# Last layer's partial results: stores split by halves of the partitions, the on-chip half laid out in pairs of groups, and two weight loads issued later

## The chip, the cores and the metric

The kernel runs on one core of a Trainium2 chip. The metric is the device time of one execution in microseconds (us); lower is better. Before the change the median of 3 runs is 1939.19 us (1938.2 to 1945.02).

The engines are TensorE (PE in the profile; PEld is its weight load), VectorE (DVE), ScalarE (ACT), GpSimd (POOL) and SyncE (SP). In this kernel SP issues nearly all transfers between HBM and on-chip memory, and 16 DMA engines carry them out.

## The reference

The input is x, 16 x 256 x 256 float32, that is 4096 tokens of 256 features. Four layers add to it in turn: a cross attention with a hard choice, a mixture of 8 experts, a cross attention with 16 heads of 64, and the one that matters here, a grouped mixture of 32 x 4 = 128 small experts:

```
b, s, d = x.shape                                   # 16, 256, 256, normalized x
g = Wc.shape[1]                                     # 32
grouped = x.reshape(b, s // g, g, d)                # 128 groups of 32 tokens
logits = einsum('bntd,des->bntes', grouped, Wc) + bc + tie
perm = (logits == max(logits, axis=-3))             # each of 128 experts picks one token of each group
permuted = einsum('bntd,bntes->bnesd', grouped, perm)
inner = relu(einsum('bnesd,esdf->bnesf', permuted, W1) + b1)       # 256 -> 32
result_permuted = einsum('bnesf,esdf->bnesd', inner, W2) + b2      # 32 -> 256
result = einsum('bnesd,bntes->bntd', result_permuted, perm)        # back to the tokens
```

## The kernel before, in words

The first 1680 us or so compute the three earlier layers. The last layer follows as one long stage.

*Choice and gather* (`pe_step`, with `dve_step`, `act_step`, `pool_step`). For each of 16 batches of 256 tokens the experts' choices are found (PMT), and TensorE gathers the chosen tokens into PX. The 128 groups of tokens fall into two halves, 64 groups each. The first half's up products run in the middle of it.

*Up products* (`pe_up`, `dve_up`). Four products per half (j = 0 to 3, 32 experts each), with W1 in the four buffers WF1P. Each signals `s_u3`, so that `s_u3` counts to 4 for the first half and to 8 for both. The result after ReLU is INT.

*Down products* (`pe_tail`). For k = 0 to 7, `down_a(k)` computes the first half's results of 16 of the 128 experts and `down_b(k)` computes the second half's results, again for 16 experts. `down_a` has groups on the partitions, `down_b` features. VectorE and ScalarE, two PSUM banks each, copy `down_a`'s result to RPA (two buffers, 1 MiB each) and `down_b`'s result to RPB (64 KiB per partition, one buffer for all k). `s_e0` and `s_e1` count these copies. `down_a(k)` waits for the RPA copies of k-1, `down_b(k)` for the RPB copies of k-1. The copy into RPA for k waits until the store of k-2 has landed (`rpa_free`).

*The way out and back for the first half.* SP stores each RPA to the scratch tensor `rpd` (64 groups, 128 experts, 256 features). A partition of RPA holds, for one of 64 groups and one of two values of a, 8 experts x 256 features, which is 8 KiB in one piece in `rpd`. Partition 64a + g is group g. The store is one transfer of 128 partitions whose destination is written as a (2), g (64), 2048 elements. After all eight stores have landed SP loads R2A(b), b = 0 to 7, with experts on the partitions, 1 MiB each, three buffers.

*The way for the second half.* RPB stays on chip, and `turn_b` transposes it, with experts on the partitions afterwards; VectorE adds b2 into R2B.

*Return* (`bias`, `back`, `out_add`, SP's `out`). TensorE brings the results back to the tokens, VectorE adds them to X, and SP stores 16 pieces of the output, 256 KiB each. The program of TensorE for i = 0 to 9 is: `turn_b(i)`, `bias(i-2)`, `back("b", i-1)`, `back("a", i-2)`, as far as these exist.

*W2.* WF2P[0 to 3] hold W2, 1 MiB each; `down_a(k)` and `down_b(k)` use WF2P[k // 2]. WF2P[2] and WF2P[3] lie where WF1P[0] and WF1P[1] were. SP's program (`sp_tail`) issues loads 0 and 1 after the last gather (`s_ga` 16), load 2 at `s_u3` 5, load 3 at `s_u3` 6, and then the stores of RPA.

The order of each engine's work is its program text, written out by hand; waits are on semaphores and nothing is reordered. Where a line of the profile names L28, it is the helper `Waits.wait_ge`.

Of the kernel before, what the change touches and what calls it, by code (L numbers as in the profile page):

```python
# [56 lines left out]
def build(nc, A, OUT):  # L57
    fp32 = mybir.dt.float32
# [8 lines left out]
    def sem(name):  # L67
        return nc.alloc_semaphore(name)
# [3 lines left out]
    PS = [nc.alloc_psum_tensor(f"ps{i}", [128, 512], fp32) for i in range(8)]  # L72
# [9 lines left out]
    rpd = nc.dram_tensor("rp_scratch", (64, 128, 256), fp32).ap()  # L82
# [4 lines left out]
    ident, ustrict, ones = CST[:, 0:128], CST[:, 128:256], CST[:, 256:384]  # L87
# [226 lines left out]
    for i in range(SLOTS0):  # L314
        g, r = i // 8, i % 8
# [35 lines left out]
    d_ks_rp = [sem(f"d_ks_rp{i}") for i in range(4)]  # L351
# [1063 lines left out]
    attn_at = mem.at  # L1415
# [73 lines left out]
    WF1P += [Arena(nc, ot1_at + 8192 * i)(f"WF1P{i + 2}", [128, 2, 32, 32], fp32) for i in range(2)]  # L1489
    RPA = [Arena(nc, ot1_at + 8192 * i)(f"RPA{i}", [128, 2, 4, 256], fp32) for i in range(2)]  # L1490
    PX = Arena(nc, attn_at)("PX", [128, 2, 128, 64], fp32)
    RPB = Arena(nc, attn_at)("RPB", [128, 2, 64, 128], fp32)

    d_c1 = sem("d_c1")
    d_wf1, d_wf2 = [sem(f"d_wf1{i}") for i in range(2)], [sem(f"d_wf2{i}") for i in range(2)]
# [4 lines left out]
    s_px, s_py, s_u3, s_in, s_b2 = sem("px_act"), sem("px_dve"), sem("upmm3"), sem("inner3"), sem("b2split")  # L1500
    s_fm, s_e0, s_e1, s_cm2, s_xo = sem("downmm3"), sem("rp0"), sem("rp1"), sem("returnmm"), sem("xout")
    TURN, LOGIT, PERM, GATHER, SMALL = PS[0], PS[1], PS[2], (3, 4, 5, 7), (0, 1, 2, 6)
    ks_sent = 32 * 16
# [12 lines left out]
    def returned(kind, b):  # L1516
        return RET.index((kind, b)) + 1

    def rpa_free(w, k):
        if k >= 2:  # L1520
            w.wait_ge(d_ks_rp[(k - 2) % 4], ks_sent + 16 * ((k - 2) // 4 + 1))

    def rpa_part(k, r):
        return RPA[k % 2][:, :, r, :], PS[SMALL[r]][:, :].rearrange("p (h d) -> p h d", h=2)

    def rpb_part(k, r):
        es = 16 * (4 * (k % 2) + k // 2) + r
        return (RPB[:, :, :, :].rearrange("p a g s -> p s (a g)")[:, es:es + 13:4, :],
                PS[GATHER[r]][:, :].rearrange("p (q n) -> p q n", q=4))

    def pe_step(e, w, n):
        def turn_choice(b):
# [73 lines left out]
    def pe_tail(e, w):  # L1606
# [37 lines left out]
        def turn_b(i):  # L1644
            for t in range(4):
                w.wait_ge(s_e0, 16)
                w.wait_ge(s_e1, 16)
                w.wait_ge(s_e0, 16 + 4 * (i - 1) + t + 1 if i else 16)
                for u in range(2):
                    for dh in range(2):  # L1650
                        c0 = u * 256 + dh * 128
                        m = e.transpose(PS[SMALL[t]][:, c0:c0 + 128], RPB[:, dh, 8 * i + 2 * t + u, :], ident)
                m.then_inc(s_fm, 1)

        def bias(b):
# [31 lines left out]
        for i in range(10):  # L1687
            if i < 8:
                turn_b(i)
            if i >= 2:  # L1690
                bias(i - 2)
            if 1 <= i <= 8:
                back("b", i - 1)
            if i >= 2:
                back("a", i - 2)
# [73 lines left out]
    def dve_tail(e, w):  # L1769
# [9 lines left out]
        for k in range(8):  # L1779
            w.wait_ge(s_fm, 2 * k + 1)  # L1780
            rpa_free(w, k)
            for r in range(2):
                i = e.tensor_copy(*rpa_part(k, r))
            i.then_inc(s_e0, 1)
            w.wait_ge(s_fm, 2 * k + 2)
            for r in range(2):
                i = e.tensor_copy(*rpb_part(k, r))
            i.then_inc(s_e0, 1)
# [27 lines left out]
    def act_tail(e, w):  # L1816
        w.wait_ge(s_om, 32)
        w.wait_ge(s_u3, 8)
        for k in range(8):
            w.wait_ge(s_fm, 2 * k + 1)  # L1820
            rpa_free(w, k)
            for r in range(2, 4):
                i = e.activation(*rpa_part(k, r), ACT.Copy)
            i.then_inc(s_e1, 1)
            w.wait_ge(s_fm, 2 * k + 2)
            for r in range(2, 4):
                i = e.activation(*rpb_part(k, r), ACT.Copy)
            i.then_inc(s_e1, 1)
# [17 lines left out]
    def sp_tail(e, w):  # L1846
        def first(j, buf):
            sent = d_kl_wf1[buf] if buf < 2 else d_wf1[j]
            e.dma_start(WF1P[buf][:, :, :, :], A["wf1"][:, :, 32 * j:32 * j + 32, :]).then_inc(sent, 16)

        def second(j):
            sent = d_wt_wf2[j] if j < 2 else d_wf2[j - 2]
            e.dma_start(WF2P[j][:, :, :].rearrange("p (a q) d -> p a q d", a=2),
                        A["wf2"].rearrange("p (a q) d -> p a q d", a=2)[:, :, 4 * j:4 * j + 4, :]).then_inc(sent, 16)

        def out(kind, b):
            n = returned(kind, b)
            t, m = 2 * (b + 8 * (kind == "b")), (n - 1) % 4
            w.wait_ge(s_xo, n)
            e.dma_start(o_v[:, t:t + 2, :], XO[m][:, :, :]).then_inc(d_x_wf2_out[m], 16)  # L1860

        def back_in(b):
            w.wait_ge(s_cm2, returned("a", b - NR) if b >= NR else 0)
            e.dma_start(R2A[b % NR][:, :, :], rpd[8 * b:8 * b + 8, :, :].rearrange("n s d -> s n d")).then_inc(d_r2[b % NR], 16)

        w.wait_ge(s_ca, 64)
        e.dma_start(WC1[:, :, :], A["wc1"]).then_inc(d_c1, 16)
        e.dma_start(BC1[:, :], A["bc1"]).then_inc(d_c1, 16)
        e.dma_start(B1[:, :], A["b1_1"]).then_inc(d_c1, 16)
        w.wait_ge(a1.s_sc, 2 * U)  # L1870
        e.dma_start(B2[:, :], A["b2_1"]).then_inc(d_c1, 16)
        first(0, 0)
        first(1, 1)
        w.wait_ge(s_om, 32)
        first(0, 2)
        first(1, 3)
        w.wait_ge(s_u3, 1)
        first(2, 0)
        w.wait_ge(s_u3, 2)
        first(3, 1)  # L1880
        w.wait_ge(s_ga, 16)
        second(0)
        second(1)
        w.wait_ge(s_u3, 5)
        second(2)
        w.wait_ge(s_u3, 6)
        second(3)
        for k in range(8):
            w.wait_ge(s_e0, 2 * k + 1)
            w.wait_ge(s_e1, 2 * k + 1)  # L1890
            e.dma_start(rpd.rearrange("g (a k y) d -> k a g (y d)", a=2, k=8)[k],
                        RPA[k % 2][:, :, :, :].rearrange("p h r d -> p (h r d)")).then_inc(d_ks_rp[k % 4], 16)
        for j in range(4):
            w.wait_ge(d_ks_rp[j], ks_sent + 16 * 2)
        w.wait_ge(s_fm, 16)
        for b in range(NR):
            back_in(b)
        for kind, b in RET:
            if kind == "a" and b + NR < 8:
                back_in(b + NR)  # L1900
            out(kind, b)
        for j in range(4):
            w.wait_ge(d_x_wf2_out[j], 16 + 16 * 4)
# [513 lines left out]
```

## Time and profile before

| what | us |
|---|---|
| median of 3 runs | 1939.19 (1938.2 to 1945.02) |
| the profiled execution's own time | 1944.29 |
| its span, first to last instruction | 1942.4 |
| TensorE matmul busy | 1717.9 (88%) |
| DVE busy | 1314.3 (68%) |
| ACT busy | 1153.3 (59%) |
| POOL busy | 822.2 (42%) |

The profile shows one execution of the program. All positions in it are microseconds from the first instruction. The granted clock of TensorE is given as a share of full speed (1.00 is 2.4 GHz, 0.50 is 1.2 GHz). "DMA share" is the mean busy share of the 16 DMA engines. Transfers are not counted as engine work: an engine that waits for one shows as idle, with the transfer named as the releaser. A float32 matmul whose operands are not transposes shows as two records.

### The profile page before, as it was taken

What the parts mean: (1) busy time and instruction counts of PE and PEld (TensorE: products, weight loads), DVE (VectorE), ACT (ScalarE), POOL (GpSimd) and SP (SyncE); (2) the same over time, 40 slices, a digit from 0 to 9 for tenths busy, and PEclk for the clock granted to TensorE, in tenths of its full rate; (3) what the DMA queues carried; (4) which work ended last, traced back from release to release, by engine and by line L of the source; (5) the groups of instructions that cost most, each with busy time, mean ns of one, the idle gap of its engine ahead of it and who ended that gap; (6) DMA issues with size and microseconds to landing.
All of it is one profiled execution on the core that took longest, in us unless ns stands there. A gap on an engine that the chain in (4) does not pass through costs nothing.

```text
span 1942.4 us, 42261 instructions
## 1 busy us (share of the span) xinstructions
PE 1717.9 (88%) x16368; PEld 1470.4 (76%) x16368; DVE 1314.3 (68%) x2802; ACT 1153.3 (59%) x2882; POOL 822.2 (42%) x1292
## 2 busy tenths in 40 slices
PE   5899999999999999999997999999999999773235
PEld 4567676788999999999996787887887887662123
DVE  4798988427058988888866777777777766641124
ACT  1477776333467777777755777777777774331100
POOL 2244532100123333333316778888888775320000
PEclk7799999999999999999998999999999999875567
DMA  6756554368766666666765222222222111221117
GB/s 176 216 116 140 120 133 96 115 220 290 255 232 245 230 235 247 251 237 230 243 239 174 63 66 88 66 67 88 66 66 88 56 53 47 89 93 54 54 54 269
DMA packets 130553, 285.02 MB, mean 147 GB/s; under 512 B 13681, under 2 KB 74353, under 8 KB 116657
## 3 DMA queue, kind: packets, MB, share of 16 engines
q1 hardware_dynamic: 110768, 174.00, 29.4%
q0 software_dynamic: 19584, 108.31, 16.1%
q8 instruction: 130, 2.13, 0.4%
q14 instruction: 71, 0.57, 0.1%
HBM read 199.95 MB, written 82.05 MB: 145 GB/s over the span
## 4 chain that ended last, share of the span: by engine, by line
PE 70%; DMA 11%; DVE 10%; POOL 4%; issue 4%; ACT 1%; SPq 0%; DVEq 0%; POOLq 0%; ACTq 0%
PE ps L1250 11%; PE ps L1236 11%; DMA rp_scratch<-RPA 8%; PE ps L1928 5%; PE ps L373 4%; PE ps L219 4%; PE ps L1959 4%; PE ps L1914 4%; PE ps L1948 4%; PE ps L379 3%; PE ps L464 2%; PE ps L440 2%; DVE NM L592 2%; POOL P L209 2%; PE ps L540 2%
## 5 line engine op out<-in xcount | busy, mean ns | idle before, releaser
L196 ACT ACTIVATE P<-ps,NM 128x256 f32<-128x256 f32 x512 | 236.7, 482 | 126.5 <-DVE NM L185 125.8
L209 POOL TENSOR_TENSOR P<-P,RS 128x1024 f32<-128x1024 f32 x128 | 243.1, 1904 | 72.1 <-DVE RS L203 71.6
L1236 PE MATMUL ps<-XRP,W1P 128*128 128x256 f32 x1872 | 226.8, 281 | 3.3 <-DVE W1P L1319 3.3
L1236 PEld LDWEIGHTS ps<-XRP,W1P 128*128 128x128 f32 x1872 | 220.1, 190 | 3.6 <-DVE W1P L1319 3.6
L1250 PE MATMUL ps<-W2P,HP 128*128 128x256 f32 x1872 | 221.5, 277 | 0.0
L1250 PEld LDWEIGHTS ps<-W2P,HP 128*128 128x128 f32 x1872 | 218.0, 188 | 0.0
L592 DVE TENSOR_REDUCE NM<-ps 128x2 f32<-128x512 f32 x256 | 164.3, 684 | 33.4 <-PE ps L440 32.3
L690 ACT ACTIVATE PT<-ps 128x512 f32<-128x512 f32 x256 | 139.2, 597 | 66.3 <-PE ps L452 63.8
L185 DVE TENSOR_REDUCE NM<-ps 128x2 f32<-128x512 f32 x256 | 164.5, 684 | 5.7 <-PE ps L1914 4.2
L1170 POOL DMA_INDIRECT WE<-in_we,WIX x39 | 44.3, 1137 | 269.2 <-DVE W1P L1319 208.8
L1279 ACT ACTIVATE HF<-ps,WE 128x256 f32<-128x256 f32 x312 | 129.1, 465 | 43.0 <-PE ps L1236 43.0
L2047 DVE CAST OT<-ps 128x256 fp32r<-128x256 f32 x128 | 54.3, 424 | 139.0 <-PE ps L1928 137.7
L1914 PEld LDWEIGHTS ps<-K,Q 64*128 64x128 f32 x1536 | 100.9, 189 | 59.7 <-issue 42.4
L226 ACT ACTIVATE PT<-ps 128x512 f32<-128x512 f32 x256 | 140.9, 618 | 0.7 <-PE ps L219 0.7
L1928 PE MATMUL ps<-PT,V 128*64 128x256 f32 x1024 | 138.8, 392 | 1.1 <-DVE OT L2049 1.1
L1914 PE MATMUL ps<-K,Q 64*128 64x256 f32 x1536 | 127.4, 299 | 10.6 <-DVE Q L2041 5.4
L219 PE MATMUL ps<-CST,P 128*128 128x128 f32 x1024 | 133.0, 273 | 3.1 <-ACT PT L226 3.1
L1270 ACT ACTIVATE W2P<-WE 128x512 fp32r<-128x512 f32 x156 | 97.2, 623 | 53.9 <-PE ps L1250 53.9
L1166 POOL DMA_INDIRECT XR<-xn_scratch,RIX x78 | 79.6, 1020 | 102.1 <-PE ps L1212 48.1
L219 PEld LDWEIGHTS ps<-CST,P 128*128 128x128 f32 x1024 | 114.4, 140 | 4.6 <-issue 3.9
L1336 DVE TENSOR_TENSOR HP<-HF,HP 128x512 fp32r<-128x512 f32 x156 | 108.0, 692 | 13.3 <-ACT HP L1286 7.1
L1948 PE MATMUL ps<-XNP,W1Q 128*128 128x256 f32 x768 | 110.4, 294 | 4.5 <-POOL XNP L2221 4.5
(234 smaller groups left out, 3765.0 us busy)
## 6 DMA issues: line engine op xcount, KB each, us to landing
KS<-k_scratch SPq DMA_DIRECT2D x64, 256.0 KB, 3.1
V<-v_scratch SPq DMA_DIRECT2D x16, 1024.0 KB, 6.3
k_scratch<-KVM SPq DMA_DIRECT2D x52, 256.0 KB
QS<-q_scratch SPq DMA_DIRECT2D x96, 128.0 KB, 4.6
v_scratch<-KVM SPq DMA_DIRECT2D x40, 256.0 KB
ys_scratch<-YS SPq DMA_DIRECT2D x39, 256.0 KB, 7.9
ctx_scratch<-CHL SPq DMA_DIRECT2D x32, 256.0 KB, 3.0
CHR<-ctx_scratch SPq DMA_DIRECT2D x16, 512.0 KB, 4.5
```

Of the source, the lines that this page charges most:

```text
L185: e.tensor_reduce(self.NM[:, u % 4, 2 * x:2 * x + 2], PS[SB[n % 3]][:, :].rearrange("p (h j) -> p h j", h=2), AX.X, ALU.max, negate=True). ...
L196: i = e.activation(self.P[u % 4][:, c, :], PS[SB[n % 3]][:, y * 256:y * 256 + 256], ACT.Exp, bias=self.NM[:, u % 4, c:c + 1], accum_out=se ...
L209: e.tensor_tensor(p, p, self.RS[:, u % 4, :].unsqueeze(2).to_broadcast([128, 4, 256]), ALU.mult).then_inc(self.s_pn, 1)
L219: i = e.transpose(PS[TB[h]][:, c0:c0 + 128], self.P[u % 4][:, c, jt * 128:jt * 128 + 128], ident)
L226: e.activation(self.PT[u % 4][h][:, :], PS[TB[h]][:, :], ACT.Copy).then_inc(self.s_tv, 1)
L592: e.tensor_reduce(NM0[b % 2][:, :, 8 * h + p], PS[SB[(2 * u + h) % 3]][:, :].rearrange("p (l j) -> p l j", l=2), AX.X, ALU.max, negate=Tru ...
L690: e.activation(PT0[u % 4][h][:, :], PS[TB[h]][:, :], ACT.Exp).then_inc(s_ex0, 1)
L1236: m = e.matmul(PS[p][:, hh * 256:hh * 256 + 256], W1P[i % 2][wi][:, cc * 1024 + hc * 128:cc * 1024 + hc * 128 + 128], XRP[i % 2][xi][:, cc ...
L1250: m = e.matmul(PS[4 + k][:, s * 256:s * 256 + 256], HP[k][hi][:, hc, s * 128:s * 128 + 128], W2P[k][wi][:, hc * 256:hc * 256 + 256], start ...
L1914: m = e.matmul(PS[SB[(2 * u + h) % 3]][:, lt * 256:lt * 256 + 256], Q1[i][64 * h:64 * h + 64, p, lt * 128:lt * 128 + 128], K1[j][64 * h:64 ...
L1928: m = e.matmul(PS[OB][64 * h:64 * h + 64, 0:256], V1[b % 2][:, jt, (2 * p + h) * 64:(2 * p + h) * 64 + 64], a1.PT[u % 4][h][:, jt * 256:jt ...
L1948: m = e.matmul(QB[:, j * 256:j * 256 + 256], W1Q[wi][:, cc, c0:c0 + 128], XNP[b % 2][xi][:, cc, :], start=(cc == 0 and x == 0), stop=(cc = ...
```

## The change

Three edits, all in the last layer. Each RPA store becomes two transfers, one for each half of the 128 partitions (a = 0, then a = 1), with groups as the outermost dimension of the destination; the semaphore targets go from 16 to 32 for each k. RPB holds the two groups 2n and 2n + 1 side by side for each expert (last dimension y), so that `rpb_part` writes and `turn_b` reads with other steps. SP's loads of WF2P[2] and WF2P[3] both wait for `s_u3` 8.

```diff
-    RPB = Arena(nc, attn_at)("RPB", [128, 2, 64, 128], fp32)
+    RPB = Arena(nc, attn_at)("RPB", [128, 2, 32, 128, 2], fp32)
@@ def rpa_free(w, k)
-            w.wait_ge(d_ks_rp[(k - 2) % 4], ks_sent + 16 * ((k - 2) // 4 + 1))
+            w.wait_ge(d_ks_rp[(k - 2) % 4], ks_sent + 32 * ((k - 2) // 4 + 1))
@@ def rpb_part(k, r)
-        return (RPB[:, :, :, :].rearrange("p a g s -> p s (a g)")[:, es:es + 13:4, :],
-                PS[GATHER[r]][:, :].rearrange("p (q n) -> p q n", q=4))
+        return (RPB[:, :, :, :, :].rearrange("p a g s y -> p s (a g) y")[:, es:es + 13:4, :, :],
+                PS[GATHER[r]][:, :].rearrange("p (q n y) -> p q n y", q=4, y=2))
@@ def turn_b(i)
-                        m = e.transpose(PS[SMALL[t]][:, c0:c0 + 128], RPB[:, dh, 8 * i + 2 * t + u, :], ident)
+                        m = e.transpose(PS[SMALL[t]][:, c0:c0 + 128], RPB[:, dh, 4 * i + t, :, u], ident)
@@ def sp_tail(e, w)
-        w.wait_ge(s_u3, 5)
+        w.wait_ge(s_u3, 8)
         second(2)
-        w.wait_ge(s_u3, 6)
         second(3)
         for k in range(8):
             w.wait_ge(s_e0, 2 * k + 1)
             w.wait_ge(s_e1, 2 * k + 1)
-            e.dma_start(rpd.rearrange("g (a k y) d -> k a g (y d)", a=2, k=8)[k],
-                        RPA[k % 2][:, :, :, :].rearrange("p h r d -> p (h r d)")).then_inc(d_ks_rp[k % 4], 16)
+            for a in range(2):
+                e.dma_start(rpd[:, 64 * a + 8 * k:64 * a + 8 * k + 8, :].rearrange("g y d -> g (y d)"),
+                            RPA[k % 2][64 * a:64 * a + 64, :, :, :].rearrange("p h r d -> p (h r d)")).then_inc(d_ks_rp[k % 4], 16)
         for j in range(4):
-            w.wait_ge(d_ks_rp[j], ks_sent + 16 * 2)
+            w.wait_ge(d_ks_rp[j], ks_sent + 32 * 2)
```

## Rows read from the trace of the kernel before

**Rows 1.** The page: the chain that ended last, share of the span by engine.
```profile
PE 70%; DMA 11%; DVE 10%; POOL 4%; issue 4%; ACT 1%; SPq 0%; DVEq 0%; POOLq 0%; ACTq 0%
```

**Rows 2.** The chain in order of time, 1743 to 1908: start us, us, what.
```profile
1743.85 2.45 DVE RPB L1787 x2
...
1747.44 37.01 DMA rp_scratch<-RPA
1784.54 1.30 DVE RPA L1783 x2
...
1864.19 37.76 DMA rp_scratch<-RPA
1902.09 5.89 DMA R2A<-rp_scratch
1908.03 1.94 PE ps L1678 x16
```

**Rows 3.** Windows of 4 us; columns in the first line.
```profile
core 0: us, PE busy (x) PEld busy (x) DVE busy (x) ACT busy (x) POOL busy (x), PEclk, DMA share, GB/s
...
1724.00:1728.00 4.00, 2.25 (x85) 2.01 (x79) 1.12 (x2) 0.00 (x0) 0.00 (x0) 0.50 1.01 378
...
1732.00:1736.00 4.00, 1.20 (x88) 1.03 (x76) 1.12 (x2) 0.00 (x0) 0.00 (x0) 1.00 0.64 247
...
1740.00:1744.00 4.00, 4.00 (x113) 2.90 (x116) 2.56 (x5) 1.24 (x3) 0.00 (x0) 0.97 0.02 4
1744.00:1748.00 4.00, 2.39 (x72) 1.93 (x59) 3.41 (x4) 3.21 (x4) 0.00 (x0) 0.89 0.13 49
1748.00:1752.00 4.00, 3.53 (x63) 2.28 (x60) 2.36 (x2) 2.37 (x2) 0.00 (x0) 0.50 0.13 53
...
1776.00:1780.00 4.00, 0.00 (x0) 0.00 (x0) 0.00 (x0) 0.00 (x0) 0.00 (x0) 0.50 0.13 53
1868.00:1872.00 4.00, 4.00 (x32) 3.67 (x34) 3.68 (x6) 0.00 (x0) 0.00 (x0) 0.75 0.13 53
1920.00:1924.00 4.00, 4.00 (x52) 2.94 (x51) 3.67 (x6) 0.00 (x0) 0.00 (x0) 1.00 1.09 379
```

**Rows 4.** Line 1045, the four 1 MiB stores of `XNF`: time to landing.
```profile
DMA to landing us min/median/max: 4.9/6.0/7.1
```

**Rows 5.** Timeline from 1720: start, length, engine, line, operation, shapes, count, idle before.
```profile
1726.91 3.44 PE L1602 MATMUL ps<-PX,WF1P 128*32 128x64 f32 x128 [1.75 <-issue]
...
1731.21 1.99 PE L1602 MATMUL ps<-PX,WF1P 128*32 128x64 f32 x128 [0.85 <-issue]
...
1737.16 2.99 PE L1602 MATMUL ps<-PX,WF1P 128*32 128x64 f32 x101 [3.96 <-issue]
...
1741.77 2.01 PE L1640 MATMUL ps<-INT,WF2P 32*128 32x64 f32 x64
...
1743.20 43.14 SPq L1891 DMA_DIRECT2D rp_scratch<-RPA  x4
...
1766.30 2.01 PE L1626 MATMUL ps<-WF2P,INT 32*64 32x256 f32 x32 [10.37 <-DVE RPA L1783]
...
1768.24 3.69 PE L1640 MATMUL ps<-INT,WF2P 32*128 32x64 f32 x64
```

**Rows 6.** Groups by shape, 1676 to 1943: busy us, mean ns, idle before.
```profile
L1787 DVE COPY RPB<-ps 128x512 f32<-128x512 f32 x16 | 16.3, 1098 | 2.9 <-PE ps L1640 2.9
...
L1783 DVE COPY RPA<-ps 128x512 f32<-128x512 f32 x16 | 10.3, 688 | 95.8 <-DMA rp_scratch<-RPA 95.2 <-PE ps L1626 0.5
...
L1709 DVE COPY PX<-ps 128x512 f32<-128x512 f32 x9 | 6.2, 687 | 7.2 <-PE ps L1571 7.2
```

**Rows 7.** Timeline from 1862, the transposes (line 1652) and the adds.
```profile
1865.99 5.63 PE L1652 MATMUL ps<-CST,RPB 128*128 128x128 f32 x32 [15.72 <-DVE RPB L1787]
...
1874.92 1.07 PE L1678 MATMUL ps<-R2B,PMT 128*32 128x256 f32 x16
...
1918.84 1.97 PE L1652 MATMUL ps<-CST,RPB 128*128 128x128 f32 x16
```

## The prediction

> **What bounds the kernel now.** I read four views, from wide to narrow. The page's chain by engine comes first: TensorE carries 70% and DMA 11% [rows 1]. TensorE's share is spread over the whole kernel, the DMA share is nearly all in one place. The chain in order of time shows that place: from 1743.20 to 1902.09 us it is one long alternation of `rp_scratch<-RPA` waits of 37 to 38 us and copies of 1.3 us [rows 2] (the first store's issue at 1743.20 is in [rows 5]). (A 37 us piece spans two of the eight stores: RPA has two buffers, so the copy of group k waits for the store of k-2.) Each store then takes (1902.09 - 1743.20) / 8 = 19.9 us for 1 MiB. The windows say why [rows 3]: with nothing else running, at 1776, the DMA engines are 0.13 busy and move 53 GB/s. 0.13 of 16 engines is 2 engines, at some 27 GB/s each. TensorE does nothing in that window. So this stage waits for two DMA engines, and the other fourteen are idle.
>
> The Trainium skill ("DMA: Bandwidth & Descriptors", section on why a DMA increments its semaphore by 16) says that the number of engines is the largest up to 16 that divides the slowest dimension of both sides. The destination here has a=2 outermost. The 0.13 agrees with 2 of 16.
>
> **Edit 1, each store as two of 64 partitions.** The outermost dimension becomes 64 on both sides. If that lets all engines work, a group's megabyte no longer takes 19.9 us. Bounds for issue to landing of 1 MiB: below, 4.9 us, the fastest of the four other 1 MiB stores of this kernel (`xn_scratch<-XNF`; 4.9/6.0/7.1) [rows 4]; above, the 19.9 us of now. Nothing in the trace shows a big transfer on 64 partitions. The nearest row is the 1 MiB store, and I take its slow end, 7.1, less a little: 7.0, issue of the second half (0.48 us, one more SP issue per group) included. SP has nothing else to do there, so eight more issues cost nothing.
>
> With stores at 7 us the loop has another bound, its own pace per group, c. Down product "b" of group k+1 waits for the RPB copies of group k, and these for product b of group k. At full clock: product b 2.01 us (the one at 1741.77), two RPB copies, handoffs of about 0.2 [rows 5]. At half clock TensorE alone takes 2.01 + 3.69 + 0.1 = 5.8 us a group (the pair at 1766.30 and 1768.24) and that hides the copies.
>
> **Edit 2, RPB in pairs of groups.** The copy now writes two neighbouring floats at each stop and not one. Now a DVE copy takes 1.10 us against 0.69 for the contiguous RPA copy. The trace has a row for writes in pairs: the PX copies (line 1709) write pairs far apart and take 0.687 us [rows 6]. Bounds 0.69 and 1.10; I take 0.69, its exact likeness. Two copies 1.4 us, so at full clock c = 2.01 + 1.4 + 0.2 = 3.6; with the old layout, whose first copies took 2.45 us [rows 2], it would be 4.7. The price is on the reading side: 128 transposes now read with a step of two floats. No row shows such a read. Not below now (same elements, same shape); above, I bound it by twice, 1.97 us more per group of 16 [rows 7]. I take nothing, and keep the other end as a rival.
>
> Which clock? TensorE's granted clock was 0.97 at 1740, 0.89 at 1744 with TensorE busy 2.39 of 4 us, and 0.50 from 1748 (0.50 is 1.2 GHz, 1.00 is 2.4 GHz); in 1868:1872, after TensorE had begun to work without a pause at 1866, it was back at 0.75, and it is 1.00 at 1920 [rows 3]. At c = 3.6 TensorE would be busy 3.1 of 3.6 us, far more than in the window before it fell; if it does fall, it is busy without a pause and may rise again. So c lies between 3.6 and 5.8, with a mix likely. Middle 4.7; I take 4.9, since the only two groups that ran undisturbed did lose the clock.
>
> Does the store fit under 4.9? RPA's copy of k+2 would like to start 2 x 4.9 - 1.3 = 8.5 us after the issue of store k; landing takes 7.0. 1.5 us to spare; each us beyond costs half a us a group, 3.5 in all.
>
> The Trainium skill has a rule against this edit ("SBUF — State Buffer", Door 1, the DMA port swizzle; also "DMA: Bandwidth & Descriptors", table of patterns): partitions 0 to 63 reach only 8 of the 16 memory ports, two transfers to the two halves serialize, and one should use one transfer of 128 partitions. By its 218 GB/s a group would take an estimated 4.8 us of transfer, just under my pace. No row here shows the 64-partition case.
>
> **Edit 3, W2 loads 2 and 3 wait for all up products.** Now the third and fourth load (1 MiB each) are issued during up products, and TensorE then stands with "issue" as the cause: 1.75 us before 1726.91 (first loads in flight, stays) and 3.96 before 1737.16, with 0.85 between these two [rows 5]. In 1732:1736 TensorE had 1.20 us of work while DMA moved 247 GB/s. 0.85 + 3.96 = 4.8 us is the most that goes. But SP now issues both loads as the down products start (2 x 0.6 us, done before the first store is due 3.1 us later), and TensorE still has to get its instructions while 2 MiB move, for some 6 us at the 378 GB/s of 1724:1728 [rows 3]. Part of the stall comes back there. Bounds: gain 4.8, loss 3. I take a gain of 2.0. The loads land some 8 us after the up products; group 4 needs them after 4 x 4.9 = 20 us. Store 0 queues behind them, and lands about 11 us after the down products start, where its buffer is wanted after 3.1 + 8.5 = 11.6: covered by 0.6 us.
>
> **The sum**, on the profiled execution (span 1942.40, its own time 1944.29):
> first store issued at 1743.20 - 2.0 = 1741.2; eighth 7 x 4.9 = 34.3 later, 1775.5 (now 1864.19); landed + 7.0 = 1782.5; first R2A load + 5.9 = 1788.4; then what follows 1908.0 now, 34.4 us to the end [rows 2], 1822.8. The 34.4 stays: in 1920:1924 TensorE is busy 4.00 of 4 us and DMA moves 379 GB/s [rows 3], so neither has slack. The transposes before R2A is there and what follows them take 10.0 us from the last RPB copy (1865.99 to 1875.99) [rows 7]; after the change they start some 2 us after the last store's issue and end 12 us after it, R2A lands 12.9 after it: just covered.
> Change 1822.8 - 1942.4 = -119.6. The profiled execution was 5 us above the median of the runs (1939.19); I see no reason for the stage to share in it, so 1939.19 - 119.6 = 1819.6, rounded 1820.
>
> **Rivals.**
> A. Fast loop: full clock throughout and stores at the full rate, c = 3.6, landing 6.0. 7 x 1.3 + 1.0 = 10 less: 1810. For it: TensorE would be busy 86% of the time. Against: landing at 6 us with 2 x 3.6 - 1.3 = 5.9 between issue and next need leaves nothing to spare. 15%.
> B. Slow loop: half clock, c = 5.8; or each half moves at half of the best rate seen, 379 / 2 = 190 GB/s, so 1.05 MB / 190 = 5.5 us a group, c = 5.5 and landing 8. +5 to +6: 1826. For the first: the clock row at 1748. The port rule of the Trainium skill is the mechanism of the second. 22%.
> C. Strided transposes cost double and TensorE, which has no slack in the last stage, stretches it by 8 x 1.97 = 16: 1836. Or TensorE's instruction supply stalls by 2 us a group beside fast stores: about the same. 10%.
> D. The change doesn't do what it says: two engines still serve each half. The two halves together take 19.9 us, edit 2 lies under the waits and only edit 3 counts: 1937. Against: every other store here has a large outermost dimension and runs wide. 3%.
> E. Slower: the number of engines goes down with the partitions, so each half is served by one. Then 8.39 MB at 27 GB/s take twice 158.9 us: +159, about 2096. It decides as soon as the stores move at less than 53 GB/s; at that rate the change is even. 2%.
> My forecast with 16 engines and c from 4.2 to 5.4: 48%, own range 1813 to 1826.
>
> **How the numbers follow.** 1820 is the likeliest case. The range leaves out D and E, and the outer parts of A and C: 1804 to 1837. A measurement of this kernel tells some 0.5% (10 us) from no change. Faster by more than that: forecast, A, B, C, 0.95; within: D, 0.03; slower: E, 0.02.
>
> **What would show it.** Right: DMA busy share far over 0.13 in the down stage, SP issues of `rp_scratch<-RPA` x16, eight groups in about 40 us and not 121 + 38; `RPB` copies near 0.69 us; no "RPA <- DMA rp_scratch" wait of more than 1 or 2 us; the transposes still at 273 ns; the "issue" gap before the last up product gone or shorter. Wrong: a landing of over 8.5 us with copies waiting for it (B's second form), a granted clock of 0.50 through the stage with groups at 5.8 (B's first), transposes over 400 ns at full clock, or a last stage well off 34.4 us. If the DMA share stays 0.13 (D) or falls to 0.06 (E), the reading of the two engines was wrong.

## The result, and the profile after

The changed kernel takes 1829.09 us, median of 4 runs (1825.11 to 1829.51), against 1942.11 (1938.2 to 1950.86, 4 runs) before: ratio 0.9408, 95% interval 0.937 to 0.9445. Predicted were 1820 (1804 to 1837) and a change of -119.6; the medians differ by 113.0.

Part of such a difference is not the change's. The first W2 load, ahead of which no variant here leaves anything out or puts anything in, was issued between 1711.95 and 1736.32 us in the 13 profiled executions. So I read the last stage from its own marks: the issue of the first W2 load, the issue of the first R2A load, and the end of the span. Before, these are 1719.05, 1902.09 and 1942.4; after, 1721.74, 1785.96 and 1827.6. The first part shrank from 183.0 to 64.2 us, the second grew from 40.3 to 41.6: together -117.5.

The chain by engine and in order of time, of the changed kernel [rows 1 and 2 before]. Columns of the second: start us, us, what.

```profile
PE 76%; DVE 10%; POOL 5%; issue 4%; DMA 4%; ACT 1%; SPq 0%; DVEq 0%; POOLq 0%; ACTq 0%
```

```profile
1746.92 1.34 PE ps L1640 x39
1748.26 1.94 PE ps L1626 x32
1750.20 3.67 PE ps L1640 x64
...
1781.74 1.30 DVE RPB L1787 x2
...
1783.08 6.68 PE ps L1652 x32
1789.76 1.00 PE ps L1678 x16
```

DMA's share of the chain fell from 11% to 4%, and the stage from store to store is now `PE ps L1626` and `PE ps L1640` in turn, without a piece of `rp_scratch<-RPA` between. The bound changed from two DMA engines to TensorE.

The same windows as [rows 3], four us each.

```profile
core 0: us, PE busy (x) PEld busy (x) DVE busy (x) ACT busy (x) POOL busy (x), PEclk, DMA share, GB/s
1740.00:1744.00 4.00, 3.60 (x102) 2.66 (x101) 2.23 (x4) 2.02 (x4) 0.00 (x0) 1.00 0.95 380
1744.00:1748.00 4.00, 2.11 (x71) 2.04 (x64) 1.55 (x3) 1.24 (x3) 0.00 (x0) 1.00 1.06 364
1748.00:1752.00 4.00, 4.00 (x78) 2.87 (x73) 2.58 (x4) 2.19 (x4) 0.00 (x0) 0.52 0.82 289
...
1764.00:1768.00 4.00, 4.00 (x76) 2.81 (x72) 2.25 (x4) 2.07 (x4) 0.00 (x0) 0.50 0.96 225
1776.00:1780.00 4.00, 4.00 (x76) 2.90 (x72) 2.58 (x4) 2.18 (x4) 0.00 (x0) 0.50 0.90 199
1796.00:1800.00 4.00, 4.00 (x51) 2.94 (x50) 3.36 (x6) 0.00 (x0) 0.00 (x0) 1.00 1.09 373
```

From 1748 to 1784 the DMA share is 0.68 to 0.96 where it was 0.13. And TensorE is busy 4.00 of 4 us at a granted clock of 0.50, that is 1.2 GHz, to the end of the down products. It was 1.00 (2.4 GHz) from 1728 until 1748.

The timeline with the up products and the first and last down products [rows 5 before].

```profile
1729.53 1.99 PE L1602 MATMUL ps<-PX,WF1P 128*32 128x64 f32 x128 [1.69 <-issue]
...
1733.00 1.99 PE L1602 MATMUL ps<-PX,WF1P 128*32 128x64 f32 x128 [1.48 <-issue]
...
1736.49 1.65 PE L1602 MATMUL ps<-PX,WF1P 128*32 128x64 f32 x101 [1.50 <-issue]
...
1740.40 0.65 PE L1626 MATMUL ps<-WF2P,INT 32*64 32x256 f32 x6 [1.23 <-issue]
...
1742.41 38.14 SPq L1891 DMA_DIRECT2D rp_scratch<-RPA  x16
...
1746.92 1.34 PE L1640 MATMUL ps<-INT,WF2P 32*128 32x64 f32 x39 [1.53 <-issue]
...
1776.04 2.01 PE L1626 MATMUL ps<-WF2P,INT 32*64 32x256 f32 x32
...
1777.98 3.69 PE L1640 MATMUL ps<-INT,WF2P 32*128 32x64 f32 x64
```

The gap of 3.96 us before the last up product is 1.50 now (the one before it grew from 0.85 to 1.48), but there are two new ones with the cause "issue": 1.23 us inside product a of group 0 and 1.53 us inside product b of group 1. From group 2 on a group takes 2.01 + 3.69 less a small overlap, 5.56 us.

What "issue" stands for is a reading. By the counts in this timeline the gaps come 127 or 128 matmuls apart (128, 128, 101 + 26, then 6 + 64 + 32 + 25), and the profile's DMA queue called "instruction" moves one packet of 0.02 MB between 1744.4 and 1745.4, just ahead of the gap of 1.53 us. That fits instructions which arrive in blocks; no run shows that it is such a block that TensorE waits for.

Groups by shape [rows 6 before]; busy us, mean ns, idle before.

```profile
L1787 DVE COPY RPB<-ps 128x512 f32<-128x512 f32 x16 | 10.3, 687 | 17.2 <-PE ps L1640 17.2
L1783 DVE COPY RPA<-ps 128x512 f32<-128x512 f32 x16 | 10.3, 686 | 5.9 <-PE ps L1626 5.9
...
L1652 PEld LDWEIGHTS ps<-CST,RPB 128*128 128x128 f32 x128 | 18.5, 212 | 4.1 <-issue 1.6 <-DVE RPB L1787 1.6 <-DVE R2B L1795 0.8
```

The RPB copies take 687 ns, as the pairs of the PX copies had said. No copy of VectorE into RPA waits for a store; the time ahead of them is TensorE's.

### The profile page after: what moved, and what is told of

Same layout as the page of the kernel before. It is cut to its first block, busy times and chain, and to the rows that moved or that the text cites. A ratio compares the mean times of both kernels' runs of the same rounds, so it can differ in the third digit from the quotient of the medians.

```text
span 1827.6 us, 42269 instructions
## 1 busy us (share of the span) xinstructions
PE 1715.0 (94%) x16368; PEld 1467.8 (80%) x16368; DVE 1310.4 (72%) x2802; ACT 1146.7 (63%) x2882; POOL 822.9 (45%) x1292
## 4 chain that ended last, share of the span: by engine, by line
PE 76%; DVE 10%; POOL 5%; issue 4%; DMA 4%; ACT 1%; SPq 0%; DVEq 0%; POOLq 0%; ACTq 0%
PE ps L1250 12%; PE ps L1236 12%; PE ps L1928 5%; PE ps L373 5%; PE ps L219 5%; PE ps L1959 4%; PE ps L1914 4%; PE ps L1948 4%; PE ps L379 4%; PE ps L464 3%; PE ps L440 2%; DVE NM L592 2%; POOL P L209 2%; PE ps L540 2%; PE ps L452 1%
```

## The experiments

"First part" is from the issue of the first W2 load to the issue of the first R2A load, "second part" from there to the end of the span, both from one profiled execution.

| run | ratio to the kernel before (95%) | first part | second part | group, us |
|---|---|---|---|---|
| before | 1 | 183.0 | 40.3 | 19.9 |
| changed kernel | 0.9408 (0.937 to 0.9445) | 64.2 | 41.6 | 5.56 |
| ctl_after | 0.9401 (0.9373 to 0.9429) | 65.1 | 39.6 | 5.56 |
| e1_split_only | 0.9433 (0.9403 to 0.9462) | 70.7 | 41.5 | 6.38 |
| e2_no_pairs | 0.9425 (0.940 to 0.945) | 70.2 | 41.7 | 6.37 |
| e3_early_w2 | 0.9388 (0.9364 to 0.9413) | 59.8 | 40.4 | 3.4 to 5.6 |
| e4_split_columns | one execution, 1946.78 us | 185.3 | 39.8 | some 20 |
| e5_burst | one execution, 1816.09 us | 63.1 | 39.2 | 5.6, then 3.4 |
| e6_w2_spaced | 0.9402 (0.9376 to 0.9427) | 65.6 | 39.6 | 5.56 |
| e7_one_store_128 | 0.9418 (0.9385 to 0.9451) | 51.9 | 55.1 | 3.42 |
| e8_linear_scratch | 0.9365 (0.9339 to 0.9391) | 53.9 | 40.9 | 3.42 |
| e9_linear_late_w2 | 0.9392 (0.9369 to 0.9414) | 63.8 | 41.0 | 5.56 |
| e10_gap | one execution, 1848.41 us | 66.5 | 43.8 | 5.56 |

**ctl_after**, the changed kernel again, beside the next three.

> The changed kernel itself, as the measure for the runs beside it. Theory (the down stage now goes at TensorE's own pace at half clock, 5.56 us a group, and no store is waited for): about 1829, -113. Rival (part of the gain belongs to one chip or one execution): off by more than 5 us.

Measured: 1834.6 where the kernel before had 1953.3 on the same chip. The time is 5.5 us over the first one's 1829.09, the ratio is the same within its interval, since the kernel before was slower there too. So only ratios, times from one chip and the parts of the profiles are compared below; in the parts the same kernel differs by 0.9 and 2.0 us.

**e1_split_only**: the kernel before with edit 1 alone (the diff's store loop and its semaphore targets).

> Edit 1 alone: old RPB layout, W2 loads 2 and 3 at s_u3 5 and 6. Theory: nearly all of the gain is the engines of the stores, DMA share in the stage from 0.13 to some 0.8; a group takes 3.69 (product b at half clock) + 2.2 (strided copies, now on TensorE's path) + 0.2 = 6.1 us and not 5.56, +3.8 over seven groups; transposes 0.22 us faster per 16, -1.8; up products stall 4.7 us longer and the down products 2.8 less: +2. Sum 1833, that is 4 us over the changed kernel. Rival (the layout and the loads lie under other work): within 1 us of the changed kernel. Rival (layout was needed to get the stage off the stores): over 1845.

**e2_no_pairs**: the changed kernel with

```diff
-    RPB = Arena(nc, attn_at)("RPB", [128, 2, 32, 128, 2], fp32)
+    RPB = Arena(nc, attn_at)("RPB", [128, 2, 64, 128], fp32)
```

and `rpb_part` and `turn_b` as before.

> The changed kernel with the old RPB layout (edits 1 and 3). Theory: copies of 1.0 to 1.2 us each, groups at 6.1 us in place of 5.56, +3.8; transposes back to 1.97 us for 16 from 2.19, -1.8; sum +2, 1831. Rival (the slower transposes weigh as much as the copies save, since TensorE has no slack in the last stage): 1828 to 1829. The PEld mean of the transposes is to go back from 0.212 to 0.157 us.

Measured: 1839.44 and 1840.77, 4.8 and 6.2 us over ctl_after in the medians, 5.6 and 5.1 in the first part. The intervals of the three ratios overlap, so what the pairs are worth is read from the first part and from the groups, not from the times. The split alone brings nearly all of the gain, -111 of -117.5 in the two parts. From e1, a product b (line 1640) in the middle and the copies by shape:

```profile
1756.65 3.69 PE L1640 MATMUL ps<-INT,WF2P 32*128 32x64 f32 x64 [0.75 <-ACT RPB L1827]
```

```profile
L1787 DVE COPY RPB<-ps 128x512 f32<-128x512 f32 x16 | 19.7, 1329 | 18.7 <-PE ps L1640 18.7
...
L1652 PEld LDWEIGHTS ps<-CST,RPB 128*128 128x128 f32 x128 | 15.2, 150 | 5.3 <-DVE RPB L1787 2.8 <-issue 2.1 <-DVE R2B L1795 0.4
```

A copy takes 1.33 us and not the 1.10 of [rows 6]: VectorE and ScalarE now start their copies in the same moment (they wait for the same product and no longer for a store), where before ScalarE mostly led by some 0.2 to 0.3 us. No run changes their starts alone, but the kernel before has both cases: its first two pairs of copies, begun together, took 2.45 and 2.46 us for two, the later ones 1.9. Product a of the next group hides 2.01 of the 2.7 us, the rest is the gap of 0.75, and a group comes to 6.38. So pairs save 0.8 us a group. They also cost what I had left as a bound: transposes of 16 blocks in 2.19 us and not 1.97, and the PEld mean is 212 against 150 ns, so it is the weight load that reads RPB with the step. Eight times 0.22 is an estimate of 1.8 us for the last stage. The second parts (41.5 and 41.7 in these two, 39.6 to 41.6 with pairs) vary too much to show it.

**e3_early_w2**: the changed kernel without edit 3.

```diff
-        w.wait_ge(s_u3, 8)
+        w.wait_ge(s_u3, 5)
         second(2)
+        w.wait_ge(s_u3, 6)
         second(3)
```

> The changed kernel with W2 loads 2 and 3 at s_u3 5 and 6 as before (edits 1 and 2). Theory (the loads stall TensorE's instruction supply wherever they are in flight, the stall is a bit larger in the up products): the up products take 19.4 us and not 14.7, the two issue gaps of 1.2 and 1.5 us in the first two down groups go; +2, 1831. Rival (the stalls have nothing to do with the loads): the gaps of 1.2 and 1.5 us stay with the loads gone from there, and the up products still take 14.7.

Measured: 1833.02 against 1834.6, unclear as a time; the first part 5.3 us shorter than ctl_after's (4.4 shorter than the changed kernel's), not 2 longer. The windows of e3 and a copy into RPA:

```profile
1756.00:1760.00 4.00, 3.64 (x125) 3.04 (x124) 2.09 (x4) 1.61 (x4) 0.00 (x0) 1.00 0.93 244
...
1768.00:1772.00 4.00, 2.85 (x89) 2.19 (x86) 2.48 (x4) 2.09 (x4) 0.00 (x0) 1.00 1.01 307
...
1776.00:1780.00 4.00, 4.00 (x79) 3.50 (x64) 1.29 (x2) 1.08 (x2) 0.00 (x0) 0.50 0.92 219
```

```profile
1773.32 1.29 DVE L1783 COPY RPA<-ps 128x512 f32<-128x512 f32 x2 [2.11 <-DMA rp_scratch<-RPA]
```

The gap of 3.69 us is back before the last up product, and the two gaps in the down products are gone, as the theory said. What neither theory had: with those gaps gone, TensorE keeps full clock into the sixth group. Groups start at 3.4 us until VectorE has to wait for a store (five times, 8.0 us in all); the last copies before the clock falls in the sixth group stand 4.6 us apart. The windows from 1756 to 1776 move 234 to 307 GB/s, 254 on average, at a DMA share of 0.79 to 1.01. So edit 3 trades a stall for the clock, and at full clock the stores are the bound.

Beside e1, e3 also says more of the pairs. Both have early loads and split stores, and differ in edit 2 alone; the first parts are 59.8 and 70.7. In e1 product b of group 1 (1745.35) waits 1.60 us for the RPB copies, and from the next product on everything runs at half clock; in e3 that wait is 0.36 and the clock stays. With late loads, where the clock goes anyway, the pairs save 5.1 us (ctl_after and e2), with early ones 10.9.

**e4_split_columns**: the kernel before, split the other way.

```diff
-            e.dma_start(rpd.rearrange("g (a k y) d -> k a g (y d)", a=2, k=8)[k],
-                        RPA[k % 2][:, :, :, :].rearrange("p h r d -> p (h r d)")).then_inc(d_ks_rp[k % 4], 16)
+            for h in range(2):
+                e.dma_start(rpd.rearrange("g (a k y) d -> k a g (y d)", a=2, k=8)[k][:, :, 1024 * h:1024 * h + 1024],
+                            RPA[k % 2][:, h, :, :].rearrange("p r d -> p (r d)")).then_inc(d_ks_rp[k % 4], 16)
```

> The kernel before, each store also in two transfers, but by columns (the two values of h, 4 KiB runs), the destination still with a = 2 outermost. Theory (the number of engines follows the outermost dimension of the destination): DMA share stays at 0.13 and the group at some 17 to 20 us, time as before within 5 us. Rival (two transfers in flight for each group are what speeds it up, whatever their shape): DMA share 0.25 and more, groups at 10 us or less, time down by 60 us or more.

Measured: one execution of 1946.78, the kernel before beside it 1944.28 (1934.32 to 1950.97). One row of e4, 40 us of the stage:

```profile
1760.00:1800.00 40.00, 11.27 (x192) 8.85 (x192) 6.20 (x8) 5.79 (x8) 0.00 (x0) 0.50 0.13 53
```

Two transfers for each group and still 0.13 and 53 GB/s. It is not their number: it is the outermost dimension of 2. The Trainium skill's rule on how many engines a transfer gets ("DMA: Bandwidth & Descriptors", why a DMA increments its semaphore by 16) agrees with this run and with edit 1.

**e5_burst**: the changed kernel, in `down_a`, ahead of the products of group 3:

```diff
+            for _ in range(24 if k == 3 else 0):
+                e.transpose(PS[SMALL[0]][:, 0:128], ident, ident)
```

> The changed kernel with 24 extra transposes of the identity (results unused) ahead of down product a of group 3, where the clock is at half. Theory (the clock was lost at a gap in TensorE's work, and the down products, busy without a pause at half clock, don't bring it back; full 128 x 128 work does, and after it the down products hold it): granted clock 1.00 within some 5 us of the burst, groups 4 to 7 then at 3.5 to 4.8 us (stores become the bound), time within 3 us of the changed kernel, the burst of some 5 us paid for. Rival (the down products can't hold full clock by themselves): the clock rises with the burst and falls back to 0.50 with the next group or two, groups at 5.56, time +4.

TensorE in e5 (line 1628 is product a, 1642 product b):

```profile
1739.09 2.01 PE L1628 MATMUL ps<-WF2P,INT 32*64 32x256 f32 x32
...
1744.69 4.25 PE L1623 MATMUL ps<-CST 128*128 128x128 f32 x24
...
1751.86 1.12 PE L1628 MATMUL ps<-WF2P,INT 32*64 32x256 f32 x32
...
1753.35 2.01 PE L1642 MATMUL ps<-INT,WF2P 32*128 32x64 f32 x64 [0.36 <-DVE RPB L1789]
...
1763.62 1.45 PE L1642 MATMUL ps<-INT,WF2P 32*128 32x64 f32 x36 [1.75 <-issue]
...
1766.95 3.69 PE L1642 MATMUL ps<-INT,WF2P 32*128 32x64 f32 x64
```

At half clock the burst begins, at full clock the next product a runs (1.12 us), and groups go at 3.4 us. They hold it until an "issue" gap of 1.75 us inside product b of group 6, and are back at half clock behind it (product b at 1766.95 takes 3.69 us again). That is both theories by turns: the down products hold full clock across short gaps (0.36, 0.82 us), and they don't win it back. The first part is 1 to 2 us shorter than in the changed kernel, burst included; the total of 1816, a single execution, owes most to what lies ahead, since its first W2 load was issued at 1711.95 already.

**e6_w2_spaced**: W2 load 2 behind the store of group 0, load 3 behind that of group 2.

```diff
-        w.wait_ge(s_u3, 8)
-        second(2)
-        second(3)
@@ in the loop of the stores
+            if k in (0, 2):
+                w.wait_ge(s_u3, 8)
+                second(2 + k // 2)
```

> The changed kernel with W2 load 2 issued behind the store of group 0 and load 3 behind that of group 2. Theory (a load in flight when TensorE needs its next instructions is what stalls it): no long issue gap in the last up product and group 0; the gaps of 1.2 to 2 us move to where the loads now are. If the clock survives them the loop goes at the stores' pace, 4.8 us or a little more with 2 MiB of loads between, 1828 to 1830 where the changed kernel has 1834; if not, at 5.56 as now, 1834. Rival (the first two loads and the stores suffice for the stalls): gaps stay where they were.

```profile
1742.69 0.66 PE L1626 MATMUL ps<-WF2P,INT 32*64 32x256 f32 x6 [0.96 <-issue]
1743.27 2.32 PE L1640 MATMUL ps<-INT,WF2P 32*128 32x64 f32 x64
```

```profile
1744.00:1748.00 4.00, 4.00 (x92) 2.81 (x88) 2.33 (x5) 2.02 (x5) 0.00 (x0) 0.60 0.65 131
```

Measured: 1828.28, ratio as the changed kernel's. The gaps in the up products stay (2.95, 0.33, 1.77 us) and one of 0.96 comes in product a of group 0; no load is in flight at these last two. The rival holds here: a load in flight is not the only thing that makes an "issue" gap. What else does I did not settle. And the clock goes all the same: product b of group 0 takes 2.32 us and not 2.01, the window has 0.60, and from 1748 it is 0.50, with no gap in group 1 at all. By the window's 0.60 it went some 0.8 us behind 1744, and the first of the late W2 loads was issued at 1745.90. So neither the gap of 1.53 us in group 1 of the changed kernel nor a late load in flight is needed for the loss; e2, where the clock is gone by group 1 without a gap in that group, says the same.

**e7_one_store_128**: e3 with another scratch layout.

```diff
-    rpd = nc.dram_tensor("rp_scratch", (64, 128, 256), fp32).ap()
+    rpd = nc.dram_tensor("rp_scratch", (128, 64, 256), fp32).ap()
@@ store of group k
+            e.dma_start(rpd[:, 8 * k:8 * k + 8, :].rearrange("p y d -> p (y d)"),
+                        RPA[k % 2][:, :, :, :].rearrange("p h r d -> p (h r d)")).then_inc(d_ks_rp[k % 4], 16)
@@ load of R2A(b) (the semaphore targets, which change with both, are left out here)
+            for a in range(2):
+                e.dma_start(R2A[b % NR][64 * a:64 * a + 64, :, :],
+                            rpd[64 * a + 8 * b:64 * a + 8 * b + 8, :, :].rearrange("n s d -> s n d")).then_inc(d_r2[b % NR], 16)
```

> W2 loads as before (at s_u3 5 and 6), scratch laid out so that each store is one transfer of 128 partitions with 128 outermost, and each R2A load two transfers of 64 partitions. Theory (64 partitions give all 16 engines but only half the rate, 220 GB/s, so the pace of 4.6 to 4.8 us in the run with early W2 loads is that of half stores): store lands in 5 us or less, copies into RPA wait for nothing, groups at 3.5 us at full clock; but the R2A loads, halves now, move at some 220 GB/s and not 350 and the last stage grows by 5 us or more. Rival (halves cost nothing, the 4.8 us is the HBM side of the writes): groups still at 4.6 or more with waits for the store, last stage unchanged at 41 us.

Windows of e7, first with stores, then with loads:

```profile
1744.00:1748.00 4.00, 3.64 (x128) 2.74 (x112) 3.06 (x6) 2.75 (x6) 0.00 (x0) 1.00 0.89 360
...
1764.00:1768.00 4.00, 3.33 (x108) 2.60 (x103) 2.72 (x5) 2.42 (x5) 0.00 (x0) 1.00 0.76 309
1780.00:1784.00 4.00, 3.98 (x44) 2.88 (x36) 3.13 (x5) 0.00 (x0) 0.00 (x0) 1.00 1.14 202
```

It shows both sides of one limit. With stores of 128 partitions the window from 1744 moves 360 GB/s at a DMA share of 0.89, no copy waits for a store, and eight groups run at 3.42 us with the clock at 1.00 throughout: first part 51.9. With the R2A loads in halves, a window of loads and output stores moves 202 GB/s with the DMA engines counted as busy as can be (1.14), where whole loads with output stores among them move 379 [rows 3]; the second part grows by 13.5 to 15.5 us, where I had expected 5 or more, and eats the gain. The Trainium skill's port rule ("SBUF — State Buffer", Door 1: a range of 64 partitions reaches 8 of 16 ports, some 218 GB/s) agrees with the 202. It is too strict for our stores: 254 on average in e3 at a mean DMA share of 0.92, against 268 to 360 in e7, where the engines had pauses (0.68 to 0.89). Both halves of a group are in flight in the stores and in the loads. So the same page's statement that two such transfers serialize ("Can I just issue two DMAs to hit both halves?") agrees with the loads, and with the stores in part only; why the two differ no run shows.

**e8_linear_scratch**: both directions whole. The scratch is (64 slots, 128 partitions, 256). A partition p = 64a + g of RPA writes slot m of its 64 at 128m + p. Read back, expert (m, a) starts at 64 x (2m + a): one constant step, so 128 partitions in one transfer, and its eight groups are 8 KiB in one piece. The price is that the last layer's experts stand in the order 2m + a.

```diff
+            e.dma_start(rpd[8 * k:8 * k + 8, :, :].rearrange("y p d -> p y d"),
+                        RPA[k % 2][:, :, :, :].rearrange("p h r d -> p (h r) d")).then_inc(d_ks_rp[k % 4], 16)
@@ load of R2A(b) (the declaration of the scratch, the semaphore targets and the W2 waits of e3 are left out here)
+                        rpd.rearrange("m (a g) d -> (m a) g d", a=2)[:, 8 * b:8 * b + 8, :]
@@ pe_up
+                                 PX[:, cc, slot(32 * j + 4 * q + r), :]      # slot(x) = 2 * (x % 64) + x // 64
@@ rpb_part
+        es = 32 * (k // 2) + 2 * r + k % 2                                   # and [:, es:es + 25:8, :, :]
@@ host layout
+EX = np.arange(128).reshape(2, 64).T.reshape(128)                            # order of Wc, bc, b2
```

> A version meant to beat both: scratch laid out as (expert slot 64, partition 128, 256) so that each store is one transfer of 128 partitions (1 KiB runs) and each R2A load one of 128 partitions (8 KiB runs); for that the last layer's experts stand in the order 2m + a (weights Wc, bc, b2 permuted, PX and RPB indexed accordingly). Pairs in RPB kept, W2 loads at s_u3 5 and 6. Theory (stores of halves were limited to half the rate, loads of halves too): from the first W2 load to the first R2A load 52 us as with the single store, and not 60 to 65; from there to the end 40 and not 55: 12 us under the changed kernel, 0.933 of the kernel before. Rival (1 KiB runs slow the stores, or the clock falls again): groups over 3.5 us, gain of 5 us or less.

SP's issues in e8, then windows (stores, loads):

```profile
1722.78 11.43 SPq L1856 DMA_DIRECT2D WF2P<-in_wf  x4
1746.37 25.77 SPq L1894 DMA_DIRECT2D rp_scratch<-RPA  x8
1776.72 1.28 SPq L1867 DMA_DIRECT2D R2A<-rp_scratch  x3
```

```profile
1764.00:1768.00 4.00, 3.64 (x124) 3.04 (x124) 3.06 (x6) 2.64 (x5) 0.00 (x0) 1.00 1.01 332
...
1784.00:1788.00 4.00, 4.00 (x52) 3.11 (x48) 3.67 (x6) 0.00 (x0) 0.00 (x0) 1.00 1.04 379
```

Measured: 1820.83, ratio 0.9365 (0.9339 to 0.9391): 0.0043 under the changed kernel's 0.9408 and 0.0036 under ctl_after's. The intervals overlap, so as a time the difference is not clear of noise; over both parts the profile has 94.8 us against 105.8 and 104.7, 11.0 and 9.9 less, where 12 were expected. Of the versions with several executions it has the lowest ratio.

**e9_linear_late_w2**: e8 with edit 3 put back.

> The same with W2 loads 2 and 3 both at s_u3 8 (edit 3). Theory (the instruction stall moves from the last up product into groups 0 and 1 of the down products, and there it costs TensorE's clock): gaps of 1 to 2 us in group 0 and 1, granted clock 0.50 from some 10 us after the down products' start, groups at 5.56 us, 8 to 12 us slower than with early loads. Rival (with fast stores the clock holds in either case; the drop was due to waits): groups at 3.5 us, same time within 2 us.

TensorE in group 1, and a window well behind it:

```profile
1746.33 2.40 PE L1643 MATMUL ps<-INT,WF2P 32*128 32x64 f32 x39 [2.35 <-issue]
```

```profile
1744.00:1748.00 4.00, 1.67 (x33) 1.67 (x34) 0.12 (x1) 0.00 (x0) 0.00 (x0) 0.68 1.03 358
1756.00:1760.00 4.00, 4.00 (x80) 3.72 (x80) 1.37 (x3) 1.17 (x3) 0.00 (x0) 0.50 0.38 132
```

Measured: 1824.79 (1824.2 to 1827.88) against 1820.83 (1812.0 to 1825.18) on the same chip, 4 us in the medians where 8 to 12 were expected, and the ranges overlap; the first part is 9.9 us longer. The theory holds in the trace: gap of 2.35 us in group 1, half clock from there, 5.56 us a group.

Long gaps are in e8 too, but ahead of other work:

```profile
1740.62 2.99 PE L1605 MATMUL ps<-PX,WF1P 128*32 128x64 f32 x101 [3.69 <-issue]
```

Behind that gap the last up product runs at half clock (2.99 us, against 1.65 for the same 101 records in e9). The clock is back by product b of group 0, which takes 2.02 us.

**e10_gap**: e8 with a pause and nothing else.

```diff
@@ down_b(k), ahead of the products
+            if k == 1:
+                w.wait_ge(d_ks_rp[0], ks_sent + 16)
```

> The version with the linear scratch and early W2 loads, in which down product b of group 1 also waits for the landing of store 0: one pause of some 2 to 4 us in TensorE's work, with its instructions at hand and no W2 load in flight. Theory (a pause of some us among these products is enough to lose the clock, and they don't win it back): granted clock 0.50 from shortly after the pause to the end of the down products, groups at 5.56 us, stage 10 us longer than in the version without. Rival (the loss comes with the instruction traffic of the W2 loads, not with the pause): the clock stays at 1.00 and only the pause itself is added.

```profile
1759.74 1.12 PE L1629 MATMUL ps<-WF2P,INT 32*64 32x256 f32 x32
1763.90 3.19 PE L1645 MATMUL ps<-INT,WF2P 32*128 32x64 f32 x64 [3.04 <-DMA rp_scratch<-RPA]
1767.01 2.01 PE L1629 MATMUL ps<-WF2P,INT 32*64 32x256 f32 x32
```

```profile
1760.00:1764.00 4.00, 0.96 (x36) 0.49 (x21) 2.36 (x4) 2.05 (x4) 0.00 (x0) 1.00 0.96 318
1764.00:1768.00 4.00, 4.00 (x88) 3.57 (x96) 0.88 (x2) 0.88 (x2) 0.00 (x0) 0.56 0.64 210
1788.00:1792.00 4.00, 4.00 (x76) 2.82 (x73) 1.92 (x4) 1.74 (x4) 0.00 (x0) 0.50 0.78 262
```

One pause of 3.04 us costs 12.6 us in the first part against e8: the pause itself, and 1.2 GHz to the end of the down products although TensorE is busy 4.00 of 4 us. So one such pause is enough to lose the clock, with no W2 load in flight. It is one execution.

## Why the prediction was right, and the step that was mis-sized

The direction, the place and the main mechanism were right; the pace of a group was not. By the steps of its sum, counted from the first W2 load (22.2 + 34.3 + 7.0 + 40.3 = 103.8 predicted, 105.8 measured):

- *Up products to the first store, "I take a gain of 2.0".* Predicted 22.2, measured 20.7 (1742.41 - 1721.74). Over all 13 profiled executions it is 22.9 to 24.2 with early loads and 20.3 to 21.6 with late ones, some 2.5 less: the size was about right. Not all of it is the stall. From before to after, the gaps up to the first store fell only from 6.56 to 5.90 us in sum; the rest is clock, since the second and the last up product took 3.44 and 2.99 us before and 1.99 and 1.65 after. The other bound, "loss 3", was for stalls in the down products, and stalls there can do a second thing, which was not priced: the clock goes and stays away.
- *Seven groups, "I take 4.9".* Predicted 34.3, measured 37.0 (eighth copy done at 1779.45, less 1742.41): the first group was quick (3.2 us between the copies into RPA), the second took 6.0 with its gap, the others 5.56. This is the mis-sized term. I had put c between 3.6 and 5.8 and expected a mix, with the clock rising again once TensorE was busy without a pause. It does not, with these products: 30 us at 4.00 of 4 and 0.50 in the changed kernel, the same in e9 and e10; e5 shows that full-size work brings it back. The rise at 1868:1872 in [rows 3], on which I had leaned, was during transposes of 128 x 128, other work than the down products. That row was there to be read. The upper end was a little off too: a pair of products at half clock overlaps by 0.07 us in [rows 5] (1766.30 + 2.01 against 1768.24), where I had added 0.1, so 5.56 and not 5.8.
- *Last store, "7.0".* Measured 6.5.
- *R2A load, and "the 34.4 stays".* 40.3 predicted, 41.6 measured (39.6 in ctl_after, the same kernel). The first 32 transposes took 6.68 us (5.63 in [rows 7]) and TensorE came to its first R2A product at 1794.2, some 2 us after the load would have landed by its 5.9: the 0.9 us by which the load was to land behind TensorE's work was used up. Most of this is this one execution: in ctl_after the same 32 took 5.58.
- *Edit 2.* Copy 0.69 right (0.687). Its worth was undervalued: the old layout costs 6.38 a group, since its copies take 1.33 us each on both engines at once and TensorE waits for them, and with early loads it costs the clock as well (e1 against e3). The read side, taken as nothing, costs 0.22 us per 16 blocks.
- *Edit 1.* Two engines to all, right (e4 excludes the number of transfers). Rival B's second form, stores of halves at half the rate, is real in kind and not in size: they do move less than whole ones (e3 against e7), but 254 GB/s and not the 190 that B had. It lies hidden in the changed kernel under TensorE's 5.56 us, and shows at once when the clock holds (e3).

That the stage came within 2.0 us of the sum is in part luck: the terms were off by -1.5, +2.7, -0.5 and +1.3, and cancel in part.

The change is 119.6 against 117.5 on the profiled executions; the medians give 113.0. Of the 4.5 between, 2.7 lie ahead of the last stage, where before began it at 1719.05 and after at 1721.74; the rest is that the profiled executions stood 2.2 and 0.3 us over their medians. And of the 9 us between 1820 and 1829, 2.9 come from the starting point: one more run moved the median before from 1939.19 to 1942.11.

The likeliest case, c from 4.2 to 5.4 with its own range of 1813 to 1826, is not what happened. Rival B's first form, half clock and c = 5.8, is (1826 there, 1829 measured), and a clock of 0.50 through the stage was on the prediction's own list of signs of being wrong. A is what edit 3 prevents, and it comes only together with whole stores (e8).

What is not settled: why there are "issue" gaps where no load is in flight (e6), and by which rule the clock is lost. The length of a gap alone does not tell. The gaps of 1.48 and 1.50 us in the up products of the changed kernel passed at 1.00, as did one of 1.36 in group 4 of e8; behind 1.53 in group 1 of the changed kernel, 2.35 (e9) and 3.04 (e10) it fell, in e3 after several of about 1 us, and in e6 in group 0, where the last gaps were 1.77 and 0.96. I take no threshold from that. Nor is it settled why the down products did not win the clock back: the up products, small too but of another shape (128*32), ran just ahead of its return in e8.

## What to carry to other kernels

When a transfer is slow, divide its rate by what one engine moves (here 27 GB/s): the quotient, and the DMA busy share times 16, tell how many engines serve it, and the outermost dimension, here the destination's, is the first suspect. Splitting by partitions gives the engines back but not the full rate (202 against 379 GB/s in windows with loads, 254 against up to 360 with stores); where the layout of the scratch can be chosen, choose it so that both the store and the load have 128 partitions at one constant step.

A stall that is "only moved" has to be priced where it lands. Ahead of the last up product, 3.69 us took the clock for one product (e8). Among down products, which did not bring it back, a gap of 2.35 us went with a first part 9.9 us longer (e9 against e8), and a pause of 3.04 us put in by hand with one 12.6 us longer (e10).

## What the runs showed of the hardware that I had not expected

- Down products (32 rows deep, 64 or 128 wide) at 1.2 GHz and busy 4.00 of 4 us stayed at 1.2 GHz for 30 us, while 24 transposes of 128 x 128 brought 2.4 GHz back within 4.25 us, and the same products then held it to group 6 (e5).
- A window with loads of 64 partitions moved 202 GB/s (e7) at a DMA share of 1.14, one with whole loads 379 at 1.04 (e8). The busy share does not tell the two apart.
- Stores of 64 partitions in pairs moved 254 GB/s on average (e3), more than the loads and less than whole stores (268 to 360, e7).
- Strided copies into the same rows by VectorE and ScalarE took 1.33 us each when they began together, 1.03 (median, VectorE) where ScalarE mostly led by 0.2 to 0.3 us, and 0.69 written in pairs of floats.
